# A three-stage transformer and Mamba kernel: norm weights folded into the MLP, W2 as three float32r products, the attention's last stores and two of its products moved

## The chip, the cores and the metric

The kernel runs on one core of one Trainium2 chip. The metric is the device time in microseconds. The core has TensorE (matmul), VectorE, ScalarE, GpSimd and SyncE (which here only issues DMA), each with its own queue of instructions; they wait for one another through semaphores. In the profile they are PE, DVE, ACT, POOL and SP; PEld is TensorE's load of a stationary operand, and a q behind a name is the engine's sequencer, where it issues a DMA.

## The reference

x has the shape (2, 64, 64, 256). Layer 0 is an attention over triples with an MLP, layer 1 a set of Mamba scans in both directions along rows and columns. The change touches layer 0 alone:

```python
out = jnp.einsum('biljh,bilhd,bljhd->bijhd', att, v1, v2)
attn_out = out.reshape(B, N, N, E) @ Wo
h = x_in + attn_out
h = _layer_norm(h, ln_agg_g, ln_agg_b)
mlp = jax.nn.relu(h @ W1 + b1) @ W2 + b2
h = mlp + h
return _layer_norm(h, ln_out_g, ln_out_b)
```

Here B = 2, N = 64, E = 256, 8 heads of d_k = 32, and W1 is 256 x 512. All is float32; the weights and biases of the norms are general, not ones and zeros.

## The kernel before

There are three blocks, one after the other, each ended by a barrier: `block_attention`, `block_mlp`, `block_mamba`.

**Attention.** The heads are taken in four pairs and the batch in two, so eight blocks c of 32 steps each; a step t makes the output rows of two i. In a step VectorE multiplies the attention weights by v2 for the first 22 of the 32 d (`DD = 22`, v2 in PSUM), GpSimd for the other ten (v2 in SBUF), both into `av[t % 2]` (line 338, `product`). TensorE multiplies that with block matrices of v1 (line 521, `rows`), in four strips of 8 d, into one of three PSUM banks. ScalarE evicts the bank into `ev` (line 699, `evict`) and, every four steps, builds the next matrices `w` (line 692). Four steps fill one half of `ev`; then SyncE stores it in 16 DMAs (`store`, line 279), one for each of 8 values d8 and 2 rows r. The very last group is stored in two parts: SyncE stores its first two steps in 16 DMAs and half of the d8 of the other two in 8; ScalarE issues the other 8 (`store_last`, line 753) after its last eviction. SyncE's queue is in order, so a group's stores start when those of the group before have been issued. Before this in ScalarE's queue, 13 loads for the MLP (`load_head`) are issued during the seventh block (c = 6).

**MLP.** The 8192 tokens are taken in 16 chunks c of 512. For a chunk TensorE multiplies by Wo (line 988), and VectorE adds x (line 1205), takes the moments and normalises (lines 1182, 1186, 1190, 1192), multiplies by the gain and adds the bias of the first norm (lines 1195, 1196), giving h. TensorE transposes h (line 999); ScalarE copies it as the high float32r part of hT (line 1098), VectorE subtracts that for the low part (line 1215). W1 is taken as three float32r products (line 1041: high by high, low by high, high by low), its own two parts made once by GpSimd (lines 951, 954). ScalarE applies b1 and the relu (line 1130), giving `hid`. W2 is one float32 product, which the profile shows as two records for each matmul (line 1053). VectorE adds b2 to h (line 1220), the product to that (line 1225), and does the second norm with gain and bias.

The order on the engines is written out by hand. VectorE: `front(c + 1)` (add x to first norm), then `back(c)` (b2, first half of the product, low part of hT for c + 1, second half, second norm). TensorE: Wo of c + 1, transposes of x1 for c - 2, W1 of c, the tiles t = 0, 1, 2 of W2 of c, the transposes of h for c + 1, the tile t = 3. ScalarE: copies of x1 for c - 2, the relus of c, with the square root for `front(c + 1)` behind the second, the copies of hT of c + 1, the square root for `back(c)`. SyncE loads and stores the chunks and, after chunks 2, 5 and 7, loads the input weights of the Mamba layers (`win`, which GpSimd splits) and the weights to be folded (`out_w`, `fcw`).

## Time and profile before

| | us |
|---|---|
| three runs, median | 2342.24 (2337.80 to 2343.77) |
| profiled execution | 2340.56 |
| its span | 2338.8 |
| PE, DVE busy | 1994.4 (85%), 1990.9 (85%) |
| ACT, POOL busy | 1264.6 (54%), 1336.7 (57%) |
| first row of the MLP block | 1084.56 |
| first row of the Mamba block | 1432.51 |

The profile is one execution. Busy shares are means over three stages with different limits, and a row of TensorE has a modelled end, so that pipelined rows overlap; the distance between starts tells the pace. The mean granted clock of TensorE is 0.978 of full speed (1.00 is 2.4 GHz, 0.50 is 1.2 GHz).

### The profile page before, as it was taken

What the parts mean: (1) busy time and instruction counts of PE and PEld (TensorE: products, weight loads), DVE (VectorE), ACT (ScalarE), POOL (GpSimd) and SP (SyncE); (2) the same over time, 40 slices, a digit from 0 to 9 for tenths busy, and PEclk for the clock granted to TensorE, in tenths of its full rate; (3) what the DMA queues carried; (4) which work ended last, traced back from release to release, by engine and by line L of the source; (5) the groups of instructions that cost most, each with busy time, mean ns of one, the idle gap of its engine ahead of it and who ended that gap; (6) DMA issues with size and microseconds to landing.
All of it is one profiled execution on the core that took longest, in us unless ns stands there. A gap on an engine that the chain in (4) does not pass through costs nothing. (4 is left out here: it accounts for less than half of the span.)

```text
span 2338.8 us, 43716 instructions
## 1 busy us (share of the span) xinstructions
PE 1994.4 (85%) x17008; PEld 1414.4 (60%) x17008; DVE 1990.9 (85%) x2292; ACT 1264.6 (54%) x3096; POOL 1336.7 (57%) x710
## 2 busy tenths in 40 slices
PE   8989976786687676664999997999999999999997
PEld 7868522242232221112787875888888888888886
DVE  4426799999999999994888884899899999999997
ACT  3337568858866882321232334656665655555652
POOL 1102699999989999992011001455655555666553
PEclk9999999999999999997999998999999999999997
DMA  7768512223231212300234222432223333433432
GB/s 234 249 207 243 151 34 57 48 50 59 62 56 21 38 29 58 71 11 24 64 105 142 71 64 62 73 83 75 73 73 85 84 82 99 102 91 95 104 93 64
DMA packets 300958, 204.00 MB, mean 87 GB/s; under 512 B 202192, under 2 KB 278992, under 8 KB 296656
## 3 DMA queue, kind: packets, MB, share of 16 engines
q1 hardware_dynamic: 282400, 146.51, 26.1%
q0 software_dynamic: 8704, 33.56, 3.9%
q10 hardware_dynamic: 9648, 21.14, 3.2%
q8 instruction: 135, 2.21, 0.4%
q14 instruction: 71, 0.58, 0.1%
HBM read 133.24 MB, written 67.90 MB: 86 GB/s over the span
## 5 line engine op out<-in xcount | busy, mean ns | idle before, releaser
L338 POOL TENSOR_TENSOR att_av<-att_att,att_v2sb 128x1280 f32<-128x1280 f32 (+1 forms) x256 | 764.6, 3003 | 43.2 <-PE att_bank L521 36.2
L338 DVE TENSOR_TENSOR att_av<-att_att,att_v2ps 128x2816 f32<-128x2816 f32 (+3 forms) x288 | 765.8, 2721 | 16.8 <-PE att_bank L521 13.6
L521 PE MATMUL att_bank<-att_av,att_w 128*32 128x512 f32 x4096 | 503.8, 601 | 224.0 <-DVE att_av L338 218.2
L521 PEld LDWEIGHTS att_bank<-att_av,att_w 128*32 128x32 f32 x4096 | 144.2, 109 | 522.5 <-issue 295.9
L1913 DVE SCALAR_TENSOR_TENSOR mb_cv<-mb_bank,mb_cw,mb_cv 128x504 f32<-128x504 f32 (+2 forms) x480 | 351.4, 732 | 60.3 <-ACT mb_cv L1707 48.8
L699 ACT ACTIVATE att_ev<-att_bank 128x512 f32<-128x512 f32 x256 | 151.8, 593 | 274.3 <-PE att_bank L521 263.5
L1512 POOL TENSOR_TENSOR mb_y_lo<-mb_y,mb_y_hi 128x1024 fp32r<-128x1024 f32 x60 | 142.6, 2398 | 258.7 <-DVE mb_S L1922 258.7
L1583 PE MATMUL mb_bank<-dt_xT_hi,dt_win_hi 128*128 128x512 f32 x576 | 233.8, 406 | 26.9 <-DVE mb_cv L1913 23.8
L1583 PE MATMUL mb_bank<-dt_xT_hi,dt_win_lo 128*128 128x512 f32 x576 | 226.3, 393 | 0.0
L1583 PE MATMUL mb_bank<-dt_xT_lo,dt_win_hi 128*128 128x512 f32 x576 | 226.2, 393 | 0.0
L1707 ACT ACTIVATE mb_cv<-mb_bank,mb_cw 128x512 f32<-128x512 f32 x160 | 110.2, 690 | 194.5 <-PE mb_bank L1583 193.0
L1518 POOL TENSOR_TENSOR mb_S<-mb_S,mb_dskip 128x512 f32<-128x512 f32 x124 | 158.1, 1294 | 9.7 <-DVE mb_S L1929 9.7
L1922 DVE TENSOR_TENSOR_SCAN mb_S<-mb_dAb,mb_inj 128x512 f32<-128x512 f32 x128 | 149.5, 1209 | 3.2 <-DMA mb_dAb<-dA_rows 3.2
L1583 PEld LDWEIGHTS mb_bank<-dt_xT_hi,dt_win_hi 128*128 128x128 f32 x576 | 109.4, 190 | 61.5 <-DVE mb_cv L1913 37.5
L1495 POOL TENSOR_TENSOR mb_inj<-mb_diag,dt_dt 128x512 f32<-128x512 f32 x128 | 129.6, 1045 | 13.1 <-DVE mb_S L1922 13.0
L1725 ACT ACTIVATE mb_xc<-mb_cv,mb_cb 128x512 f32<-128x512 f32 x128 | 91.5, 715 | 69.7 <-DVE mb_cv L1913 69.7
L1643 PE MATMUL mb_bank<-dt_wf_hi,mb_y_hi 128*128 128x256 f32 x512 | 128.7, 291 | 0.0
L642 ACT ACTIVATE att_raw<-att_raw,att_least 128x64 f32<-128x64 f32 x384 | 128.1, 336 | 0.4
L1643 PE MATMUL mb_bank<-dt_wf_lo,mb_y_hi 128*128 128x256 f32 x512 | 125.9, 285 | 0.0
L1583 PEld LDWEIGHTS mb_bank<-dt_xT_hi,dt_win_lo 128*128 128x128 f32 x576 | 109.0, 189 | 24.4
L1583 PEld LDWEIGHTS mb_bank<-dt_xT_lo,dt_win_hi 128*128 128x128 f32 x576 | 109.3, 190 | 19.7
L1053 PE MATMUL mlp_bank<-mlp_w,mlp_hid 128*128 128x256 f32 x512 | 118.4, 382 | 2.9 <-ACT mlp_hid L1130 2.9
(200 smaller groups left out, 3941.8 us busy)
## 6 DMA issues: line engine op xcount, KB each, us to landing
att_xin<-in_x SPq DMA_DIRECT2D x32, 512.0 KB, 4.5
qk_t<-att_qk POOLq DMA_DIRECT2D x16, 1024.0 KB, 5.1
v<-att_vs POOLq DMA_DIRECT2D x16, 1024.0 KB, 5.9
mb_dAb<-dA_rows SPq DMA_DIRECT2D x32, 512.0 KB, 6.3
mb_dAb<-dA_cols SPq DMA_DIRECT2D x32, 512.0 KB, 5.7
mixed_t<-att_ev SPq DMA_DIRECT2D x1008, 8.0 KB
att_q<-qk_t ACTq DMA_DIRECT2D x32, 256.0 KB, 4.4
att_kb<-qk_t ACTq DMA_DIRECT2D x64, 128.0 KB, 3.0
```

What stands on the lines that cost most here:

```text
L338: return eng.tensor_tensor(av[t % 2][:, :, d0:d1, :], a.unsqueeze(2).broadcast_to((P, 2, d1 - d0, N)), v2.unsqueeze(1).broadcast_to((P, 2, ...
L521: mm = pe.matmul(bank[t % NB][s * M:(s + 1) * M, :], w[k % 2][:, i0 // 2, r, s, :], av[t % 2][:, r, s * STRIP_D:(s + 1) * STRIP_D, :], sta ...
L642: ins = act.activation(a, a, ACT.Exp, scale=-1.0, bias=least[:, j, h:h + 1], accum_out=rsum[:, j, h:h + 1])
L699: act.activation(ev[e % 2][:, step % EB, :], bank[t % NB][:, :], ACT.Copy).then_inc(o_copied, 1)
L1053: mm = pe.matmul(OUT_[t // 2][:, (t % 2) * E:(t % 2 + 1) * E], hid[:, k, t * P:(t + 1) * P], w2[:, k, :], start=(i == 0), stop=(i == FT - 1))
L1495: pool.tensor_tensor(inj[:, p], diag[:, :].unsqueeze(1).broadcast_to((P, NH, L)), dtt[way(c)][:, c % NCHUNK * PAIR + p, :].unsqueeze(2).br ...
L1512: pool.tensor_tensor(y_["lo"][:, s, :], y[:, s, :], y_["hi"][:, s, :], ALU.subtract).then_inc(y_lo_ready, 1)
L1518: pool.tensor_tensor(S[:, p, :], S[:, p, :], dskip[way(c)][:, :, :].rearrange("p h t -> p (h t)"), ALU.add)\
L1583: mm = pe.matmul(PR_[b][:, :], win_[w][:, k, col:col + P], xT_[x][:, k, :], start=(n == 0), stop=(n == 3 * KT - 1))
L1643: pe.matmul(O_[t][:, 0:E], y_["hi"][:, m, t * P:(t + 1) * P], wf[way(c)][wn][:, m, :], start=(m == 0 and wn == "hi"), stop=False)
L1913: dve.scalar_tensor_tensor(out=dst, in0=src, scalar=cw[way(c)][:, m, TAPS - 1 - back:TAPS - back], in1=dst, op0=ALU.mult, op1=ALU.add)\
L1922: dve.tensor_tensor_scan(S[:, p, :], dAb[:, p, :], inj[:, p].rearrange("p h t -> p (h t)"), 0.0, ALU.mult, ALU.add).then_inc(scanned, 1)
```

## The change

In the attention's last block (c = 7), ScalarE makes the products of the last two d (`NA = 2`), during the steps from 6 on of the block before, into the memory of q and kb, which is free by then; GpSimd leaves these two out, and VectorE takes 21 d rather than 22 at every odd step but the first and last. TensorE then multiplies strip 3 in a part of six d and two of one. The last stores are shared differently: the second to last group is split by r between SyncE and ScalarE (8 DMAs each), and each of the last four steps is stored by itself, four DMAs from SyncE and four from ScalarE, which it issues between its evictions.

In the MLP, the gain g1 and bias be1 of the first norm are folded: W1 is scaled by g1 along its rows, be1 times W1 is added to b1 (by TensorE, once), and the residual is h * g1 + (b2 + be1), h now being without them. W2 is split into two float32r parts and hid too: ScalarE applies the relu twice (high part, float32), and VectorE subtracts. Some tiles share memory (`w1g` lies in `win`, the fold weights in w1, w2 and `win`), with waits for it on SyncE.

```diff
+            if t // (N // 2) == NC - 1 and 0 < t % (N // 2) < N // 2 - 1:
+                return DD - 1 - t % 2
             return DD
         def d_of_pool(t):
-            return DK
+            return DK - (NA if t // (N // 2) == NC - 1 else 0)
...
+                    n_av = STRIP_D - (NA if s == STRIPS - 1 and c == NC - 1 else 0)
                     for r in (0, 1):
-                        mm = pe.matmul(bank[t % NB][s * M:(s + 1) * M, :],
+                        mm = pe.matmul(bank[t % NB][s * M:(s + 1) * M, 0:n_av * N],
                                        w[k % 2][:, i0 // 2, r, s, :],
-                                       av[t % 2][:, r, s * STRIP_D:(s + 1) * STRIP_D, :], start=(r == 0), stop=(r == 1))
+                                       av[t % 2][:, r, s * STRIP_D:s * STRIP_D + n_av, :], start=(r == 0), stop=(r == 1))
+                    for a in range(STRIP_D - n_av):
+                        if step == 0 and a == 0:
+                            pe.wait_ge(av_by_act, NA)
+                        for r in (0, 1):
+                            mm = pe.matmul(bank[t % NB][s * M:(s + 1) * M, (n_av + a) * N:(n_av + a + 1) * N],
+                                           w[k % 2][:, i0 // 2, r, s, :],
+                                           by_act[a][:, 2 * step + r, :], start=(r == 0), stop=(r == 1))
...
             def store(c, e):
+                if c * NE + e == NC * NE - 1:
+                    for step in range(N // 2 - EB, N // 2):
+                        sp.wait_ge(o_copied, c * (N // 2) + step + 1)
+                        for d8 in range(STRIP_D // 2):
+                            store_step(sp, step, d8)
+                    return
+                sp.wait_ge(o_copied, c * (N // 2) + (e + 1) * EB)
+                for d8 in range(STRIP_D):
+                    for r in range(1 if c * NE + e == NC * NE - 2 else 2):
+                        store_rows(sp, c, e, d8, r)
...
+            def products(step):          # ScalarE, behind evict, block NC - 2
+                lo = 3 * (step - FIRST)
+                if step == FIRST:
+                    act.wait_ge(scored, PAIRS * NG)
+                    act.wait_ge(v2_loaded, NC * 32)
+                for j in range(max(0, lo), min(lo + 3, N)):
+                    for a in range(NA):
+                        ins = act.activation(by_act[a][:, :, j], att[(PAIRS - 1) % 2][:, (B - 1) * N:B * N, j], ACT.Copy,
+                                             scale=v2in[:, j, DK - NA + a:DK - NA + a + 1])
+            def store_last(step):        # ScalarE, behind evict, block NC - 1
+                if step == N // 2 - EB - 1:
+                    act.wait_ge(o_copied, NC * (N // 2) - EB)
+                    for d8 in range(STRIP_D):
+                        store_rows(act, NC - 1, NE - 2, d8, 1)
+                if step >= N // 2 - EB:
+                    act.wait_ge(o_copied, (NC - 1) * (N // 2) + step + 1)
+                    for d8 in range(STRIP_D // 2, STRIP_D):
+                        store_step(act, step, d8)
...
+            pool.wait_ge(cols_loaded, 32)
             for k in range(KT):
-                pool.tensor_copy(w1_["hi"][:, k], w1[:, k]).then_inc(w1_split, 1)
+                pool.tensor_tensor(w1g[:, k], w1[:, k], g1c[:, k:k + 1].broadcast_to((P, F)), ALU.mult).then_inc(w1_scaled, 1)
+            for k in range(KT):
+                pool.wait_ge(w1_scaled, k + 1)
+                pool.tensor_copy(w1_["hi"][:, k], w1g[:, k]).then_inc(w1_split, 1)
...
+            pool.tensor_copy(w2_["hi"][:, :, :], w2[:, :, :]).then_inc(w2_split, 1)
+            pool.wait_ge(w2_split, 1)
+            pool.tensor_tensor(w2_["lo"][:, :, :], w2[:, :, :], w2_["hi"][:, :, :], ALU.subtract).then_inc(w2_split, 1)
...
                 for t in range(TT):
-                    for i, k in enumerate(ORDER):
-                        if t == 0:
+                    for n, (hn, wn, i, k) in enumerate([(hn, wn, i, k) for hn, wn in (("hi", "hi"), ("hi", "lo"), ("lo", "hi"))
+                                                        for i, k in enumerate(ORDER)]):
+                        if t == 0 and n < FT:
                             pe.wait_ge(hid_ready, FT * c + i + 1)
-                        mm = pe.matmul(OUT_[t // 2][:, (t % 2) * E:(t % 2 + 1) * E], hid[:, k, t * P:(t + 1) * P],
-                                       w2[:, k, :], start=(i == 0), stop=(i == FT - 1))
+                        if t == 0 and hn == "lo":
+                            pe.wait_ge(hid_lo_ready, FT * c + i + 1)
+                        mm = pe.matmul(OUT_[t // 2][:, (t % 2) * E:(t % 2 + 1) * E], hid_[hn][:, k, t * P:(t + 1) * P],
+                                       w2_[wn][:, k, :], start=(n == 0), stop=(n == 3 * FT - 1))
...
             times_wo(0, 0)
+            pe.wait_ge(cols_loaded, 32)
+            for m in range(FT):
+                for k in range(KT):
+                    mm = pe.matmul(OUT_[0][:, m:m + 1], w1[:, k, m * P:(m + 1) * P], be1c[:, k:k + 1],
+                                   start=(k == 0), stop=(k == KT - 1))
+            mm.then_inc(b1_done, 1)
...
-                    act.activation(hid[:, m, :], HID_[m][:, :], ACT.Relu, bias=b1[:, m:m + 1]).then_inc(hid_ready, 1)
+                    act.activation(hid_["hi"][:, m, :], HID_[m][:, :], ACT.Relu, bias=b1f[:, m:m + 1])
+                    act.activation(hid[:, m, :], HID_[m][:, :], ACT.Relu, bias=b1f[:, m:m + 1]).then_inc(hid_ready, 1)
...
+            def low_of_hid(c):
+                for i, m in enumerate(ORDER):
+                    dve.wait_ge(hid_ready, FT * c + i + 1)
+                    dve.tensor_tensor(hid_["lo"][:, m, :], hid[:, m, :], hid_["hi"][:, m, :], ALU.subtract)\
+                        .then_inc(hid_lo_ready, 1)
...
             def front(c, u):
-                layer_norm(0, c, chain, h[u], h[u], row["g1"], row["be1"], h_ready)
+                normed_rows(0, c, chain, h[u], h[u]).then_inc(h_ready, 1)
...
             def back(c, u):
-                dve.tensor_tensor(hb[u][:, :, :], h[u][:, :, :], wide(row["b2"]), ALU.add).then_inc(b2_added, 1)
+                dve.tensor_tensor(hb[u][:, :, :], h[u][:, :, :], wide(row["g1"]), ALU.mult).then_inc(h_scaled, 1)
+                dve.wait_ge(h_scaled, c + 1)
+                dve.tensor_tensor(hb[u][:, :, :], hb[u][:, :, :], wide(row["b2"]), ALU.add).then_inc(b2_added, 1)
...
             for c in range(NCHUNK):
                 if c + 1 < NCHUNK:
                     front(c + 1, 1 - c % 2)
+                low_of_hid(c)
                 back(c, c % 2)
```

## Rows read from the trace of the kernel before

**Rows 1.** Busy us by window: PE, PEld, DVE, ACT, POOL, clock, DMA; MLP
```profile
1200.00:1450.00 250.00, 232.38 (x1270) 189.62 (x1268) 197.91 (x434) 88.85 (x187) 18.95 (x18) 0.97 0.28 87
```

**Rows 2.** Timeline of TensorE, two chunks: start, length, operation, idle before
```profile
1248.20 4.73 PE L1053 MATMUL mlp_bank<-mlp_w,mlp_hid 128*128 128x256 f32 x20 [0.28 <-ACT mlp_hid L1130]
1252.77 1.04 PE L999 MATMUL mlp_bank<-mlp_ident,mlp_h 128*128 128x128 f32 x8
...
1276.70 5.27 PE L988 MATMUL mlp_bank<-mlp_wo,mlp_att 128*128 128x256 f32 x16 [2.46 <-DMA mlp_xin<-in_x]
```

**Rows 3.** Timeline of VectorE, one chunk
```profile
1243.99 1.28 DVE L1205 TENSOR_TENSOR mlp_h<-mlp_bank,mlp_xin 128x512 f32<-128x512 f32 x2
...
1249.31 1.22 DVE L1195 TENSOR_TENSOR mlp_h<-mlp_h,mlp_g 128x1024 f32<-128x1024 f32 x1
1250.56 1.22 DVE L1196 TENSOR_TENSOR mlp_h<-mlp_h,mlp_be 128x1024 f32<-128x1024 f32 x1
1251.82 1.22 DVE L1220 TENSOR_TENSOR mlp_hb<-mlp_h,mlp_b 128x1024 f32<-128x1024 f32 x1
1253.08 0.69 DVE L1225 TENSOR_TENSOR mlp_hb<-mlp_bank,mlp_hb 128x512 f32<-128x512 f32 x1
1254.03 1.29 DVE L1215 TENSOR_TENSOR mlp_hT_lo<-mlp_bank,mlp_hT_hi 128x512 fp32r<-128x512 f32 x2 [0.26 <-ACT mlp_hT_hi L1098]
1255.57 0.69 DVE L1225 TENSOR_TENSOR mlp_hb<-mlp_bank,mlp_hb 128x512 f32<-128x512 f32 x1 [0.25 <-PE mlp_bank L1053]
...
1262.69 1.28 DVE L1205 TENSOR_TENSOR mlp_h<-mlp_bank,mlp_xin 128x512 f32<-128x512 f32 x2
```

**Rows 4.** Timeline of ScalarE, same chunk
```profile
1247.48 1.25 ACT L1130 ACTIVATE mlp_hid<-mlp_bank,mlp_b 128x512 f32<-128x512 f32 x2
```

**Rows 5.** Timeline of TensorE in the Mamba block, a float32r product of 256 columns
```profile
1605.35 2.08 PE L1650 MATMUL mb_bank<-dt_wf_hi,mb_y_lo 128*128 128x256 f32 x16
```

**Rows 6.** Groups on VectorE: count, busy us, mean ns, idle before
```profile
L1952 DVE TENSOR_TENSOR mb_sq<-mb_sq 128x512 f32<-128x512 f32 x32 | 22.2, 692 | 1.1
```

**Rows 7.** Timelines of VectorE, SyncE and ScalarE at the attention's end
```profile
1047.87 18.20 DVE L338 TENSOR_TENSOR att_av<-att_att,att_v2ps 128x2816 f32<-128x2816 f32 x8
...
1056.75 25.51 SPq L279 DMA_DIRECT2D mixed_t<-att_ev  x40
...
1068.25 0.60 ACT L699 ACTIVATE att_ev<-att_bank 128x512 f32<-128x512 f32 x1 [2.53 <-PE att_bank L521]
1068.87 1.20 ACTq L753 DMA_DIRECT2D mixed_t<-att_ev  x1
1068.87 6.18 ACTq L753 DMA_DIRECT2D mixed_t<-att_ev  x8
1084.56 0.10 POOL L947 MEMSET mlp_eps<- 128x1 f32 x1 [19.46 <-POOLq L2072]
```

**Rows 8.** Timeline of ScalarE in the attention, scaled copies of 64 elements
```profile
859.90 2.01 ACT L654 ACTIVATE att_raw<-att_raw,att_rsum 128x64 f32<-128x64 f32 x8
```

**Rows 9.** Timeline of the MLP's first chunk
```profile
1086.52 2.49 POOL L954 TENSOR_TENSOR mlp_w_lo<-mlp_w,mlp_w_hi 128x512 fp32r<-128x512 f32 x2
...
1098.07 1.23 DVE L1196 TENSOR_TENSOR mlp_h<-mlp_h,mlp_be 128x1024 f32<-128x1024 f32 x1
1099.35 1.97 PE L999 MATMUL mlp_bank<-mlp_ident,mlp_h 128*128 128x128 f32 x8 [8.65 <-DVE mlp_h L1196]
```

**Rows 10.** Timelines of VectorE and GpSimd while GpSimd splits the input weights
```profile
1231.33 3.67 POOL L965 CAST dt_win_hi<-mlp_win 128x1152 fp32r<-128x1152 f32 x2 [48.34 <-DMA mlp_win<-in_mv_in_wT]
1231.95 2.05 DVE L1220 TENSOR_TENSOR mlp_hb<-mlp_h,mlp_b 128x1024 f32<-128x1024 f32 x1
```

**Rows 11.** Busy us by window, with the granted clock ahead of the DMA share
```profile
1058.00:1064.00 6.00, 3.90 (x38) 1.14 (x34) 6.00 (x4) 1.19 (x2) 5.87 (x3) 1.00 0.06 13
1277.00:1279.00 2.00, 2.00 (x6) 1.55 (x6) 1.56 (x5) 0.27 (x1) 0.00 (x0) 0.50 0.01 4
```

**Rows 12.** Timeline of TensorE, W2 of the last chunk
```profile
1404.55 7.07 PE L1053 MATMUL mlp_bank<-mlp_w,mlp_hid 128*128 128x256 f32 x32
```

88 lines of the change are left out of this document (57 added, 31 removed).

## The prediction

> **What bounds the kernel now.** I read the busy table by stage first, then the timelines of single chunks on each engine, then the queues. The page gives TensorE 85% and VectorE 85% of the span, which says nothing of a stage; the windows over the MLP do: of 250 us, TensorE is busy 232 and VectorE 198 [rows 1]. So TensorE looks like the bound, and the timeline of one chunk is needed. VectorE's loop runs from one add of Wo's product to the next, 1243.99 to 1262.69, 18.70 us, with its instructions back to back but for short waits, among them 0.26 before the low part of hT and 0.25 before the second half of W2's product [rows 3]. TensorE's work comes to nearly the same and has 0.28 us of idle time [rows 2]; its busy share is also made of modelled matmul ends. The reader should see here two engines of equal length where the order on VectorE closes the loop. An instruction added to VectorE lengthens a chunk; time taken from TensorE alone doesn't shorten it.
>
> At the end of the attention it is another resource. VectorE's product for two i takes 3.0 us a step when a few are followed (18.20 us over the last, merged), and the last eviction starts at 1068.25, but SyncE issues 40 stores in 25.51 us from 1056.75 to 1082.26, 0.64 us each, and the MLP's first row is at 1084.56 [rows 7]. Its queue, not the arithmetic, ends that stage.
>
> **The change, part by part.** Sums are against the profiled execution, 2340.56 us (span 2338.8 and 1.76 around it); the median of the three runs is 2342.24, 1.68 above it.
>
> *Attention, last block of 32 steps.* ScalarE makes the products of two of the 32 d, GpSimd two fewer, VectorE one fewer (21 for 22) at the 15 odd steps between first and last. One d of 22 is 1/22 of 3.0 us = 0.136; 15 x 0.136 = -2.0 us. GpSimd's share falls from 10 d to 8 or 9, so it stays below VectorE. ScalarE's 128 activations of 64 elements lie in the block before, six a step; eight comparable ones take 2.01 us [rows 8], so 1.5 us a step beside an eviction of 0.60 and now and then a build, in 3 us: hidden, at most a step late now and then, with three PSUM banks as cover (0 to +1 us). TensorE adds eight short records a step to a step with 1 us of slack: 0.
>
> *The tail's stores.* Count from the end of the eviction of step 27, when the second to last group of stores starts (1056.75). Before, SyncE has 16 + 16 + 8 issues: 25.5 us. After, it has 8, then 4 behind each of the steps 28 to 31; ScalarE has 8, then 4 behind each of its evictions, and its next eviction stands behind those issues in order. ScalarE's eight issues took 6.18 us with SyncE's beside them, the first 1.2 [rows 7], so one costs 0.7 and the first of a group 0.5 more. ScalarE: 8 issues 1.2 + 7 x 0.67 = 5.9 us, then four times (eviction 0.62 + issues 1.2 + 3 x 0.66) = 3.8 us, end at 21.1. SyncE's last four wait for the eviction of step 31 at 18 and end at 20.5. The gain is 25.5 - 21.1 = 4.4 us. Bounds: if evictions came on time (12.1 us after step 27), SyncE would end at about 14.7, a gain of 10.8; if ScalarE's issues all cost 0.75, it is 3. I take -4.3, since the queue order is certain.
>
> *MLP, start.* The first norm's gain and bias are gone: 2.5 us of the way to the first transposes, which begin at 1099.35, behind the bias at 1098.07 [rows 9]. Ahead of it GpSimd now waits for two small loads, scales W1 (two of its 512-wide operations, 2.49 us [rows 9]), splits it, and splits W2 (twice the width): from the loads' landing some 11 us, before either is wanted, since the transposes and a product with Wo stand ahead. TensorE's 16 records for b1 fall in its idle time before 1099.35. But GpSimd now works beside the first norm, and VectorE's operation on two SBUF tensors rose to 2.05 us from 1.22 when GpSimd ran [rows 10, 3]. I add 1.0 (0 to 2.5): -1.5 in all.
> The Trainium skill, "GPSIMD Engine Reference", Specifications, says the same of the pair: it shares its SBUF interfaces with VectorE, and they contend when VectorE has two SBUF inputs. By it the new subtraction, SBUF alone, is exposed too, where the loads of W_in are split; the trace bears it out for the same kind of operation, and it would add under 1 us there.
>
> *MLP, each chunk on TensorE.* W2 was 32 records of 256 columns a chunk, 7.07 us [rows 12], 0.217 each. It becomes 48 float32r records. The same form (stationary 128x128, 256 columns, float32r) runs 16 in 2.08 us, 0.12 each [rows 5]: 48 x 0.12 = 5.8. TensorE gains 1.2 us a chunk. Were the weight load, whose record lasts 0.19, to set the pace, it would lose 2.2.
>
> *MLP, each chunk on VectorE.* Removed: gain and bias of the first norm, 1249.31 to 1251.82, 2.51 us. Added: h times g1, 1.26, and four subtractions of 512. The nearest row is a 512-wide operation from SBUF, 692 ns alone [rows 6]; back to back two of that size take 1.28 to 1.30 [rows 3], so 0.60 each, 2.45 with the last's end. Net +1.2.
>
> *The order.* The subtractions stand between front(c+1) and back(c), and TensorE can't pass its first tile of W2 before the last of them; h of chunk c+1 is transposed two tiles later. Call T the end of the last subtraction. TensorE: 0.15, then 12 + 12 records at 0.12, so the transposes start at T + 3.05; from the start of the transposes to the low part of hT is 1.26 (1252.77 to 1254.03 [rows 2, 3]): T + 4.3. VectorE has 1.26 + 1.26 + 0.69 = 3.2 us of work until then, and waits 1.1 us where it waited 0.26. The loop, from the add of Wo's product: front without gain and bias 7.83 - 2.51 = 5.32; subtractions 2.45; to the low part of hT 4.3; from there to the next add 1262.69 - 1254.03 = 8.66, less the wait of 0.25 that may fall away, 8.5. Sum 20.6 us against 18.70: +1.9. ScalarE's four extra relus, 0.56 each [rows 4], fit: the square root of the next norm stands between them, at about T - 4.3, and after it come four passes of 0.56, so the last hid is ready near T - 2, before VectorE asks for it. If that were late by one pass it would cost 0.5.
> From the second add to the last there are 13 such periods, and one of start-up that TensorE sets (+0.7): 13 x 1.9 + 0.7 = +25.4.
>
> *What stalls the loop now and won't then.* At 1276.70 TensorE waited 2.46 us for a load of x beside the fold weights, and its next 16 records took 5.27 us where 16 x 0.22 = 3.5 are due [rows 2]; 4.2 us in all. With 1.9 us more in a chunk the load is nearly in time: -3.5 (0 to -4).
>
> *End.* After the last front the chain is subtractions of chunk 14, W1, one pass of relu more, and three tiles of W2 at 1.44 each instead of the whole at 0.217: +1.5.
>
> *TensorE's clock.* After the wait of 2.46 us it was granted 0.50, its lower level of 1.2 GHz; in the attention, busy 3.90 of 6 us, it kept 1.00 [rows 11, 2]. The new loop leaves TensorE 3 us of idle time a chunk, in pieces of 1.0, 1.0, 0.3 and 0.5 us with single records between, all in the 4 us ahead of T. That stands between the two rows. A fall costs about 1.4 us of the loop, since it hits the way from T to the transposes. I count one or two chunks: +2.
>
> Sum: -2.0 - 4.3 - 1.5 + 25.4 - 3.5 + 1.5 + 2.0 = +17.6; 2340.56 + 17.6 = 2358.2 profiled, and 2342.24 + 17.6 = 2359.8 as a median. I say 2360.
>
> **Rivals.**
> 1. *The clock falls in most chunks.* The low part's late arrival makes TensorE run single records with gaps for 4 us, every chunk at the same place. 13 to 14 chunks x 1.4 = 19, less the 2 counted: 2377. For it: the half clock behind one gap of 2.46 us. Against: the attention's regular gaps. 0.13.
> The Trainium skill, "TensorE: Matmul & The Clock Gate", section "A second HAM failure mode: psum-queue depth-cycling", describes it: frequent short idles between groups of matmuls make the clock switch to and fro. By that rule this rival holds; the attention's rows don't bear it out.
> 2. *The other side: the stores pay for the loop.* If ScalarE's issues return at once, so that its evictions aren't held, the tail gives 10.8 rather than 4.3; and if TensorE's first tile overtakes so that VectorE has no stall at the low part of hT, the loop grows by the net work of 1.2 alone. The place that decides is the queue of ScalarE behind step 27: the kernel isn't slower from the point where the tail gives 10 us and a chunk costs no more than 1.2. Then -2.0 - 10.8 - 2.5 + 13 x 1.2 + 0.7 - 3.5 + 1.5 = -1.0: 2341. For it: both queues idle otherwise. Against: issue durations are on ScalarE's row. 0.15.
> 3. *TensorE is the bound after all.* Then a chunk shrinks by 1.2: 15 x -1.2 = -18, with -2.0 - 4.3 - 1.5: 2316. For it: 232 of 250 us busy. Against: VectorE's loop has no room for 1.2 more. 0.05.
> 4. *The weight load paces the three products.* 48 x 0.19 = 9.1 a chunk; three tiles at 2.3 before and behind the transposes put 1.7 us more ahead of the low part and as much behind: 15 x 2.5 = 37 more, 2397. Against: the row at 0.12. 0.03.
> 5. *The change doesn't do what it says*, a part of its tail or its products on ScalarE falling on the path (c = 6 evictions late by a step each time): +5 to +10, 2367. 0.06, inside the range.
>
> **How the numbers follow.** Forecast 0.58, rivals 0.13, 0.15, 0.05, 0.03, 0.06. A change under 0.3% (7 us) can't be told from none: 2335.2 to 2349.3. Faster: rival 3 and a part of 2, 0.08. Same: the rest of 2 and the lower edge of the forecast, 0.14. Slower: 0.78. The forecast's own range is 2350 to 2369 (tail 3 to 10.8, stall 0.8 to 1.4 a chunk, start 0 to 2.5). The range that holds 8 in 10 reaches to the edge of rival 2 and to rival 1: 2343 to 2379.
>
> **What would show it.** Right: the add of Wo's product every 20.4 to 20.8 us; W2's records 0.12 apart; VectorE idle 1.1 us ahead of the low part of hT on ScalarE's copy; subtractions 0.6 apart; the MLP's first row 6 us earlier, at 1078; ScalarE's evictions of steps 28 to 31 each 3.8 us apart. Wrong: a pitch of 18.7 or less (TensorE was the bound), of 22 with half clock ahead of the transposes (rival 1), or a first row of the MLP before 1073 (rival 2).

## The result and the profile after

The changed kernel takes 2358.56 us as a median of four runs (2357.69 to 2362.40), the kernel before 2340.99 in runs beside it (2337.80 to 2343.77): ratio 1.0079, 95% interval 1.0064 to 1.0094, so 18.5 us slower. The forecast was 2360. Two executions used below stood far outside the others, one of kernel 3 (3271 us at a mean granted clock of 0.55) and one of the kernel before beside kernels 9 to 12 (3406 us at 0.64); the ratios leave them out, the printed median of 3 counts its own. The profiled execution took 2357.77 us with a span of 2356.0, which is 17.2 us above the profiled one of before; the ledger below is made between those two.

| stretch (profiled executions) | before | after | measured | forecast |
|---|---|---|---|---|
| attention to the eviction of step 27 | 1056.12 | 1050.30 | -5.8 | -2.0 |
| from there to the MLP's first row | 28.4 | 24.1 | -4.3 | -4.3 |
| MLP's first row to the second add of Wo's product | 21.73 | 20.38 | -1.35 | -1.5 |
| second to last such add, 14 chunks | 274.45 | 301.09 | +26.6 | +25.4 - 3.5 + 2.0 = +23.9 |
| last add to Mamba's first row | 51.77 | 55.75 | +4.0 | +1.5 |
| Mamba | 906.3 | 904.3 | -1.9 | 0 |

A chunk of the MLP on VectorE, timeline of the kernel after (start, length, group, idle time ahead and who ended it), which answers to [rows 3]:

```profile
1289.34 1.28 DVE L1295 TENSOR_TENSOR mlp_h<-mlp_bank,mlp_xin 128x512 f32<-128x512 f32 x2
...
1293.23 1.38 DVE L1278 TENSOR_SCALAR mlp_h<-mlp_h,mlp_mv,mlp_rstd 128x256 f32<-128x256 f32 x4
1294.64 2.50 DVE L1285 TENSOR_TENSOR mlp_hid_lo<-mlp_hid,mlp_hid_hi 128x512 fp32r<-128x512 f32 x4
1297.06 1.22 DVE L1311 TENSOR_TENSOR mlp_hb<-mlp_h,mlp_g 128x1024 f32<-128x1024 f32 x1
1298.31 1.23 DVE L1313 TENSOR_TENSOR mlp_hb<-mlp_hb,mlp_b 128x1024 f32<-128x1024 f32 x1
1299.57 0.69 DVE L1318 TENSOR_TENSOR mlp_hb<-mlp_bank,mlp_hb 128x512 f32<-128x512 f32 x1
1301.55 1.29 DVE L1306 TENSOR_TENSOR mlp_hT_lo<-mlp_bank,mlp_hT_hi 128x512 fp32r<-128x512 f32 x2 [1.29 <-ACT mlp_hT_hi L1181]
...
1309.91 1.28 DVE L1295 TENSOR_TENSOR mlp_h<-mlp_bank,mlp_xin 128x512 f32<-128x512 f32 x2
```

The reader should see the forecast's path in it: 20.57 us from add to add (20.6 forecast, 18.70 before), the subtractions in 2.50, and a wait of 1.29 us (1.1 forecast, 0.26 before) for the high part of hT. The same chunk on TensorE, which answers to [rows 2]:

```profile
1295.27 0.39 PE L1129 MATMUL mlp_bank<-mlp_w_hi,mlp_hid_hi 128*128 128x256 f32 x1 [0.77 <-ACT mlp_hid L1216]
1295.50 0.64 PE L1129 MATMUL mlp_bank<-mlp_w_lo,mlp_hid_hi 128*128 128x256 f32 x4
...
1297.20 0.38 PE L1129 MATMUL mlp_bank<-mlp_w_hi,mlp_hid_lo 128*128 128x256 f32 x1 [0.22 <-DVE mlp_hid_lo L1285]
1297.42 0.63 PE L1129 MATMUL mlp_bank<-mlp_w_hi,mlp_hid_hi 128*128 128x256 f32 x4
1297.89 0.64 PE L1129 MATMUL mlp_bank<-mlp_w_lo,mlp_hid_hi 128*128 128x256 f32 x4
...
1300.29 1.03 PE L1070 MATMUL mlp_bank<-mlp_ident,mlp_h 128*128 128x128 f32 x8
```

Four records every 0.47 to 0.48 us, 0.12 each as forecast, and the transposes 3.15 us behind the end of the last subtraction at 1297.14 (3.05 forecast). That pace holds at full clock. In four chunks it is 0.85 us for four records over a stretch; windows of the kernel after at such a place, over the loop, and over the loop of the kernel with fillers described below (columns as in [rows 1], the granted clock behind POOL):

```profile
1254.90:1258.10 3.20, 3.20 (x17) 3.20 (x16) 2.27 (x3) 0.00 (x0) 0.00 (x0) 0.50 0.00 0
1096.00:1395.00 299.00, 268.72 (x1661) 223.75 (x1659) 253.28 (x567) 117.23 (x239) 26.29 (x12) 0.98 0.27 84
```
```profile
1094.00:1390.00 296.00, 286.37 (x1927) 248.17 (x1925) 255.13 (x568) 118.24 (x241) 26.67 (x12) 1.00 0.27 85
```

The granted clock falls to 0.50 (1.2 GHz) four times in the loop of 14 chunks, at 1125.1, 1189.9, 1254.8 and 1360.6; before, once, at 1276.5. VectorE in the chunk of the third fall:

```profile
1251.62 2.50 DVE L1285 TENSOR_TENSOR mlp_hid_lo<-mlp_hid,mlp_hid_hi 128x512 fp32r<-128x512 f32 x4
...
1260.03 1.29 DVE L1306 TENSOR_TENSOR mlp_hT_lo<-mlp_bank,mlp_hT_hi 128x512 fp32r<-128x512 f32 x2 [2.37 <-ACT mlp_hT_hi L1181]
```

From the end of the last subtraction to the low part of hT it is 5.91 us, against 4.41 in the chunk at 1289.34 (4.3 forecast). So it is in all four: 5.70, 5.91, 5.91 and 5.91, while nine of the other ten chunks have 4.41 or 4.42 and one 4.81. A fall in the loop lengthens this one path, by 1.3 to 1.5 us.

The attention's end on ScalarE and SyncE, and the MLP's first row, which answer to [rows 7]:

```profile
1050.30 0.60 ACT L729 ACTIVATE att_ev<-att_bank 128x512 f32<-128x512 f32 x1 [2.14 <-PE att_bank L551]
1050.92 6.56 ACTq L235 DMA_DIRECT2D mixed_t<-att_ev  x8
1057.59 0.60 ACT L729 ACTIVATE att_ev<-att_bank 128x512 f32<-128x512 f32 x1 [6.69 <-issue]
1058.21 2.92 ACTq L242 DMA_DIRECT2D mixed_t<-att_ev  x4
1061.18 0.60 ACT L729 ACTIVATE att_ev<-att_bank 128x512 f32<-128x512 f32 x1 [3.00 <-issue]
...
1069.00 2.91 ACTq L242 DMA_DIRECT2D mixed_t<-att_ev  x4
```
```profile
1050.92 5.38 SPq L235 DMA_DIRECT2D mixed_t<-att_ev  x8
1058.21 13.32 SPq L242 DMA_DIRECT2D mixed_t<-att_ev  x16
```
```profile
1074.43 0.10 POOL L1011 MEMSET mlp_eps<- 128x1 f32 x1 [16.12 <-POOLq L2172]
```

The evictions of steps 28 to 31 stand behind ScalarE's issues (the idle time ahead of them is "issue"), 3.59 us apart where 3.8 was forecast. SyncE's row of 16 is merged and holds three waits of about 1 us for the next eviction; its first four alone:

```profile
1058.21 2.55 SPq L242 DMA_DIRECT2D mixed_t<-att_ev  x4
```

VectorE's products in the last block, groups by form (count, busy us, mean ns):

```profile
L359 DVE TENSOR_TENSOR att_av<-att_att,att_v2ps 128x2688 f32<-128x2688 f32 x15 | 44.3, 2955 | 0.0
L359 DVE TENSOR_TENSOR att_av<-att_att,att_v2ps 128x2560 f32<-128x2560 f32 x15 | 42.3, 2822 | 0.0
...
L359 DVE TENSOR_TENSOR att_av<-att_att,att_v2ps 128x2816 f32<-128x2816 f32 x1 | 3.1, 3090 | 0.0
```

2816, 2688 and 2560 elements are 22, 21 and 20 d. This shows that my working, and the text ahead of it, misread one line: `DD - 1 - t % 2` gives VectorE 21 d at even steps and 20 at odd ones, not 22 and 21, so that GpSimd has 9 and 10 and not 8 and 9. Its ten d take 2.93 us (groups of 1280 elements), a little over VectorE's 2.82 for twenty.

### The profile page after: what moved, and what is told of

Read it like the earlier page. It is cut to its first block and busy times, and to the rows that moved or that the text cites. A ratio compares the mean times of both kernels' runs of the same rounds, so it can differ in the third digit from the quotient of the medians.

```text
span 2356.0 us, 45040 instructions
## 1 busy us (share of the span) xinstructions
PE 2000.0 (85%) x17536; PEld 1445.9 (61%) x17536; DVE 2003.7 (85%) x2342; ACT 1339.0 (57%) x3288; POOL 1337.4 (57%) x714
## 5 line engine op out<-in xcount | busy, mean ns | idle before, releaser
L359 POOL TENSOR_TENSOR att_av<-att_att,att_v2sb 128x1280 f32<-128x1280 f32 (+3 forms) x256 | 759.3, 2985 | 41.7 <-PE att_bank L544 34.7
L359 DVE TENSOR_TENSOR att_av<-att_att,att_v2ps 128x2816 f32<-128x2816 f32 (+4 forms) x288 | 759.9, 2702 | 15.8 <-PE att_bank L544 12.6
L544 PE MATMUL att_bank<-att_av,att_w 128*32 128x512 f32 (+1 forms) x4096 | 502.9, 598 | 216.7 <-DVE att_av L359 204.5
L1595 POOL TENSOR_TENSOR mb_inj<-mb_diag,dt_dt 128x512 f32<-128x512 f32 x128 | 129.8, 1048 | 13.0 <-DVE mb_S L2022 12.9
L1730 PEld LDWEIGHTS mb_bank<-mb_S,mb_xtok 64*64 64x64 f32 x4096 | 107.9, 137 | 13.4 <-issue 10.9
```

The lines of the kernel that those rows point to most:

```text
L359: return eng.tensor_tensor(av[t % 2][:, :, d0:d1, :], a.unsqueeze(2).broadcast_to((P, 2, d1 - d0, N)), v2.unsqueeze(1).broadcast_to((P, 2, ...
L544: mm = pe.matmul(bank[t % NB][s * M:(s + 1) * M, 0:n_av * N], w[k % 2][:, i0 // 2, r, s, :], av[t % 2][:, r, s * STRIP_D:s * STRIP_D + n_a ...
L1595: pool.tensor_tensor(inj[:, p], diag[:, :].unsqueeze(1).broadcast_to((P, NH, L)), dtt[way(c)][:, c % NCHUNK * PAIR + p, :].unsqueeze(2).br ...
```

## The experiments

Each kernel is the one before or the changed one with the edit given. Each ratio is taken to runs of the kernel before beside that kernel (medians 2339.34 for 1 to 4, 2340.99 for 5 to 8, 2340.94 for 9 to 12); time to the kernel before is the ratio less 1, times 2341. A pitch is the time from the first add of Wo's product of one chunk to that of the next, and the usual pitch is what most undisturbed chunks have. "Loop" is from the second to the last add of Wo's product, 14 chunks, in the profiled execution; "falls" is how often the granted clock went to 0.50 within it. In the expectations, theory A is the account that I held before the run.

| kernel | median us | ratio (95%) | to before | loop | usual pitch | falls |
|---|---|---|---|---|---|---|
| before | 2340.99 | 1 | | 274.5 | 18.70 | 1 |
| changed | 2358.56 | 1.0079 (1.0064 to 1.0094) | +18.5 | 301.1 | 20.59 | 4 |
| 1 attention alone | 2329.93 | 0.9957 (0.9943 to 0.9971) | -10.1 | 275.0 | 18.70 | 1 |
| 2 stores alone | 2335.41 | 0.9982 (0.9972 to 0.9991) | -4.2 | 274.4 | 18.70 | 1 |
| 3 MLP alone | 2374.62 | 1.0137 (1.0117 to 1.0158) | +32.1 | 308.3 | 20.57 or 22.07 | 8 |
| 4 fold alone | 2333.41 | 0.9975 (0.9965 to 0.9984) | -5.9 | 270.7 | 18.70 | 0 |
| 5 split of W2 alone | 2441.30 | 1.0430 (1.0415 to 1.0444) | +100.7 | 370.6 | 24.4 to 26.1 | 14 |
| 6 transposes early | 2345.39 | 1.0024 (1.0014 to 1.0033) | +5.6 | 290.5 | 19.72 | 3 |
| 7 fillers | 2355.32 | 1.0055 (1.0042 to 1.0068) | +12.9 | 296.0 | 20.58 | 0 |
| 8 low part on GpSimd | 2355.13 | 1.0060 (1.0048 to 1.0073) | +14.0 | 300.5 | 19.6 to 22.7 | 7 |
| 9 MLP alone, fillers | 2362.00 | 1.0084 (1.0070 to 1.0098) | +19.7 | 297.5 | 20.59 | 1 |
| 10 no subtractions | 2341.47 | 1.0001 (0.9992 to 1.0010) | +0.2 | 286.8 | 19.63 | 2 |
| 11 attention and fold | 2324.37 | 0.9926 (0.9913 to 0.9939) | -17.3 | 270.6 | 18.70 | 0 |
| 12 as 11, loads spread | 2322.00 | 0.9914 (0.9900 to 0.9928) | -20.1 | 269.3 | 18.70 | 0 |

**1 and 2: the attention's parts.** 1 has the changed `block_attention`, the whole of that part of the diff, and everything else as before. 2 takes this back of it, so that only the stores are changed:

```diff
-            if t // (N // 2) == NC - 1 and 0 < t % (N // 2) < N // 2 - 1:
-                return DD - 1 - t % 2
-            return DK - (NA if t // (N // 2) == NC - 1 else 0)
+            return DK
-                if c == NC - 2:
-                    products(step)
```

> Only the attention's edits (ScalarE's products of two d, one d fewer for VectorE and two for GpSimd, the last stores on two queues); the MLP as before. Theory A, from the profile of the changed kernel (VectorE's steps in the last block 2.80 us for 3.00, so -5.8; 23.5 us from the eviction of step 27 to the MLP for 27.8, so -4.3): -10, 2331. Rival, the terms as predicted (-2.0 and -4.3): -6.3, 2335. Rival, the attention's gain comes back as waits in the MLP: no change.

> Only the stores of the attention's end are shared between SyncE and ScalarE; nobody multiplies other d than before. Theory A: -4.3 us, with ScalarE's evictions of steps 28 to 31 some 3.6 us apart and 23.5 us from the eviction of step 27 to the MLP's first row. Rival: with steps of 3.0 us the evictions come later anyway, and the gain is 5 or more; or, if the two queues slow each other's issues, under 2.

Both came out as theory A has it, 2 by its trace above all (24.0 us from the eviction of step 27 to the MLP's first row, for 28.4 before), since its interval reaches from -6.6 to -2.1. The MLP's first row is at 1074.74 in 1, at 1080.70 in 2 and at 1084.56 before: 3.9 us for the stores and 6.0 for the steps. In 2 the evictions behind ScalarE's issues are 3.5 to 3.7 us apart, as in the changed kernel; by then the shorter steps don't matter.

**3 and 9: the MLP alone, and with fillers.** 3 is the changed kernel with the attention of before. 9 adds the fillers of 7:

```diff
+                        if t == 0 and c > 0 and n in FILL:      # {2: 7, 3: 7, 9: 2, 10: 2, 11: 2}
+                            for _ in range(FILL[n]):
+                                pe.matmul(OUT_[1][:, E:2 * E], hid_["hi"][:, ORDER[0], 0:P], w2_["hi"][:, 0, :],
+                                          start=True, stop=True)
                         if t == 0 and n < FT:
                             pe.wait_ge(hid_ready, FT * c + i + 1)
```

> Only the MLP's edits (norm folded, W2 as three float32r products); the attention as before. Theory A: loop +26.6, end +4.0, start -1.4, so +27 to +29: 2369. If the two parts add up, this one and the attention's alone make +17.6. Rival: the falls of TensorE's clock depend on when the MLP starts, and without them it is +20.

> The kernel with only the MLP's edits (before's attention), with the same fillers in TensorE's idle time. It had 9 falls of the clock in the loop and 308.3 us from the second add of Wo's product to the last, where the changed kernel with the same MLP had 4 and 301.1. Theory A (the falls are all that differs between those two loops): no falls, loop 296 as in the changed kernel with fillers, -12 us to 2374.6, 2362. Rival (something else of the attention's end is carried into the loop): loop 300 or more, 2367 to 2370.

3 was slower than expected by its middle value, 32.1 us over before; its interval, +27.4 to +37.0, still touches the expected +27 to +29. With the attention's -10.1 it makes +22.0 where both together have +18.5. Its MLP instructions are those of the changed kernel, yet its loop is 7.2 us longer. Eight stretches at half clock stand in it rather than four (the nine of the expectation above count one behind the last add), and undisturbed chunks with one take 22.07 instead of 20.57. The mean granted clock is 0.973 in each of the four executions behind its ratio, and 0.975 to 0.977 in the changed kernel's four, so this is not one odd profile. Windows over the loops of 3 and of 9:

```profile
1104.00:1410.00 306.00, 274.38 (x1662) 229.54 (x1661) 255.03 (x567) 116.16 (x238) 26.35 (x12) 0.95 0.27 82
```
```profile
1104.00:1401.00 297.00, 287.84 (x1924) 249.38 (x1923) 254.38 (x568) 118.76 (x242) 26.44 (x12) 0.99 0.27 85
```

With fillers one fall is left, in the first of the 14 chunks, and the loop takes 297.5: 10.8 us less for seven falls, and a median of 2362.0 where 2362 was expected. In chunks 3, 8, 12 and 14 of the loop a fall costs 1.48 to 1.50. Not all of the 10.8 is the clock: in chunk 4 of kernel 3, 23.54 us for 21.08 in 9, GpSimd splits `win` while VectorE subtracts, and the four subtractions take 3.45 us for 2.50. So the two loops of one MLP differed mostly by the clock, and by 1 to 2 us through this, chunk 5 being late too. Why the clock fell in other chunks when the MLP began 9.5 us later isn't settled.

**4: the fold alone.** The changed MLP with W2 and hid as they were, and the attention of before:

```diff
-                    act.activation(hid_["hi"][:, m, :], HID_[m][:, :], ACT.Relu, bias=b1f[:, m:m + 1])
-                low_of_hid(c)
...
-                        mm = pe.matmul(OUT_[t // 2][...], hid_[hn][:, k, t * P:(t + 1) * P], w2_[wn][:, k, :], ...)
+                        mm = pe.matmul(OUT_[t // 2][...], hid[:, k, t * P:(t + 1) * P], w2[:, k, :], ...)
```

> Only the first norm's gain and bias are folded into W1 and b1; W2 stays one float32 product, and there is no low part of hid; the attention as before. VectorE's chunk loses 2.51 us and gains 1.26 (h times g1): 18.70 - 1.25 = 17.45 us; TensorE's work of 18.4 us a chunk would bind then. Theory A: pitch 18.4 to 18.5, -3 us over the loop, -1.4 at the start, and the stall at the fold weights' load stays: -4 to -6, 2336. Rival (VectorE's loop alone set the pace): -1.25 x 14 - 1.4 = -19, 2323. Rival: no change, since gaps move elsewhere.

Theory A holds as far as the sum goes; its pitch was to fall to 18.4 or 18.5 and stayed at 18.70. That the loop is 3.7 us shorter all the same comes from chunks that stood out before (22.81 to 21.07 us at the late load of x, 20.19 to 19.15, 19.88 to 19.25), so the sum was met in part by luck. TensorE's waits over 14 chunks, of this kernel and of the one before (total, times, longest), and one chunk's rows on VectorE here:

```profile
PE mlp_bank L1069 <- ACT mlp_hid L1155: 2.3, 4, 1.4
PE mlp_bank L1004 <- DMA mlp_xin<-in_x: 2.3, 1, 2.3
```
```profile
PE mlp_bank L1053 <- ACT mlp_hid L1130: 2.9, 6, 1.4
PE mlp_bank L988 <- DMA mlp_xin<-in_x: 2.5, 1, 2.5
```
```profile
1250.53 1.29 DVE L1245 TENSOR_TENSOR mlp_hT_lo<-mlp_bank,mlp_hT_hi 128x512 fp32r<-128x512 f32 x2 [1.52 <-ACT mlp_hT_hi L1121]
```

With 1.25 us of VectorE's work gone, VectorE waits 1.52 us where it waited 0.26, and the chunk is as long as before. VectorE's work didn't set the pitch, then. TensorE waited 6.2 us in the 14 chunks before and 4.6 here, next to nothing: it was the bound of the loop before, with VectorE, which waited 0.26 and 0.25 us in a chunk [rows 3], close behind. No run shortened TensorE's work alone, so TensorE's part rests on these waits.

**5: the split alone.** The changed MLP with W1 and b1 unscaled and the attention of before, and

```diff
-                normed_rows(0, c, chain, h[u], h[u]).then_inc(h_ready, 1)
+                chain.link(normed_rows(0, c, chain, h[u], h[u]))
+                chain.link(dve.tensor_tensor(h[u][:, :, :], h[u][:, :, :], wide(row["g1"]), ALU.mult))
+                dve.tensor_tensor(h[u][:, :, :], h[u][:, :, :], wide(row["be1"]), ALU.add).then_inc(h_ready, 1)
...
-                dve.tensor_tensor(hb[u][:, :, :], h[u][:, :, :], wide(row["g1"]), ALU.mult).then_inc(h_scaled, 1)
```

> Only W2 as three float32r products with the subtractions on VectorE; the first norm keeps gain and bias, the attention is as before. Theory A (the path from the last subtraction over three tiles of W2 and the transposes to the low part of hT sets the chunk): 7.83 to the end of the norm, 2.45 of subtractions, 4.3 to the low part of hT, 8.5 to the next add, 23.1 us, with 2.4 us of waiting ahead of the low part: +4.4 x 14 = +62 and what falls of TensorE's clock add, 2405. Rival (VectorE's work alone counts, its waits being slack): 18.7 + 2.45 - 0.26 = 20.9 us, +31, 2370.

Slower than both. The clock fell in all 14 chunks, and for longer. The window over the loop, then two rows that stand side by side in the fourth chunk:

```profile
1106.00:1470.00 364.00, 301.17 (x1641) 248.36 (x1640) 277.29 (x570) 113.88 (x234) 26.18 (x12) 0.86 0.22 69
```
```profile
1198.76 3.10 DVE L1223 TENSOR_TENSOR mlp_hid_lo<-mlp_hid,mlp_hid_hi 128x512 fp32r<-128x512 f32 x1
1198.26 3.06 POOL L985 TENSOR_TENSOR dt_win_lo<-mlp_win,dt_win_hi 128x1152 fp32r<-128x1152 f32 x1
```

Theory A's path is there piece by piece: 7.83 to the subtractions in ten of the 14 chunks, 2.50 for them in twelve, 8.36 from the low part of hT to the next add in eight and at most 9.15 in the others. With 4.42 from the last subtraction to the low part of hT that makes 23.1, and 14 x 23.1 = 323 of the 370.6 us. The other 47 us are in three places. From the last subtraction to the low part of hT it is 5.7 to 7.2 us in every chunk, partly at half clock, 28 us in all over 14 x 4.42. In chunks 4 and 7 GpSimd splits `win` beside the subtractions, which take 9.10 and 6.80 us for 2.50, 11 us more in all. The last 8 us are elsewhere, 3.6 of them in the first chunk. That the 28 us are the clock's rests on the length of the same path at full clock in the changed kernel, 4.41; no run took the falls away here.

**6: transposes early.** The changed kernel with

```diff
-                    if t == 2:
-                        turn_h(c + 1, 1 - u)
+                        if t == 0 and n == 2 * FT:
+                            turn_h(c + 1, 1 - u)
                         if t == 0 and hn == "lo":
```

> The changed kernel, but h of the next chunk is transposed in the first tile of W2, ahead of its four products with the low part of hid, not behind the third tile. Theory A: VectorE's wait of 1.29 us ahead of the low part of hT goes, its own work of 19.3 us a chunk is what is left: pitch 19.3 to 19.5 for 20.59, 14 x 1.2 = -17 to the changed kernel, 2342. Rival (TensorE's queue sets the pace): the transposes delay the first tile by as much as they bring, pitch 20.2 or more, 2353 to 2359.

Pitch 19.72, a little over theory A's, and 13 us faster than the changed kernel (5.6 over before for 18.5), where theory A had 17. Rows of a chunk:

```profile
1252.20 1.28 DVE L1306 TENSOR_TENSOR mlp_hT_lo<-mlp_bank,mlp_hT_hi 128x512 fp32r<-128x512 f32 x2
1253.96 0.69 DVE L1318 TENSOR_TENSOR mlp_hb<-mlp_bank,mlp_hb 128x512 f32<-128x512 f32 x1 [0.48 <-PE mlp_bank L1131]
```

The wait of 1.29 is gone and one of 0.48 for the second half of W2's product has come: 1.29 - 0.48 = 0.8, near the 0.87 that the pitch fell by.

**7: fillers.** The changed kernel with the edit of 9.

> The changed kernel with idle TensorE time ahead of the subtractions' end filled: 7, 7, 2, 2 and 2 products of 256 columns a chunk whose result is overwritten, put before the waits. Theory A (the falls of the clock to 0.50 in the loop cost 1.5 us each and come from that idle time): no falls in the loop, -6 us to the changed kernel, 2353. Rival: the falls stay and the fillers in front of a product cost up to 0.1 us a chunk, 2359 to 2361.

No falls, and the loop 5.1 us shorter, 1.3 for each of the four falls. The median is 3.2 us lower, the ratio 5.6, and the intervals of the ratios overlap; that TensorE's idle time caused the falls rests on the granted clock and on 9, where the difference is four times as large.

**8: the low part on GpSimd.** The changed kernel; the subtractions moved to GpSimd, and (the edits on GpSimd, SyncE and in VectorE's `low_of_hid` are left out here)

```diff
+                products(0, 0, 2 * FT)                  # tile, from product, to product
+                products(2, 0, 2 * FT)
+                turn_h(c + 1, 1 - u)
+                products(0, 2 * FT, 3 * FT)
+                products(1, 0, 3 * FT)
+                products(2, 2 * FT, 3 * FT)
+                products(3, 0, 3 * FT)
...
+                low_of_hT(c + 1, 1 - u)                 # VectorE, ahead of both adds
                 for half in range(2):
                     dve.wait_ge(w2_done, 2 * c + half + 1)
```

> The changed kernel with the subtractions for hid's low part on GpSimd, the products with the high part of hid of tiles 0 and 2 ahead of the transposes of h, and these ahead of all products with the low part; the low part of hT comes ahead of both adds of W2's product; GpSimd's split of W_in is spread over chunks 4 to 12 and its loads moved behind it (W_in's second at chunk 7, the fold weights at 12). Theory A: VectorE loses 2.45 us a chunk, and the chain norm, relus, GpSimd's last subtraction, products, add, norm makes 18.0 us: -2.6 x 14 = -36 to the changed kernel, 2322. Rival (VectorE's operations on two SBUF tensors slow down beside GpSimd, 2.05 us for 1.22, for two or three a chunk): pitch 19.5 to 20.5, 2343 to 2357.

The rival by the time, though the pitch is 19.6 to 22.7 for its 19.5 to 20.5, with seven falls of the clock among them. VectorE and GpSimd side by side, first in a chunk where GpSimd also casts a part of `win`, then in one where it only subtracts:

```profile
1207.52 2.33 DVE L1296 TENSOR_SCALAR mlp_h<-mlp_h,mlp_mv,mlp_rstd 128x256 f32<-128x256 f32 x4
1209.89 2.19 DVE L1323 TENSOR_TENSOR mlp_hb<-mlp_h,mlp_g 128x1024 f32<-128x1024 f32 x1
1212.12 2.05 DVE L1325 TENSOR_TENSOR mlp_hb<-mlp_hb,mlp_b 128x1024 f32<-128x1024 f32 x1
```
```profile
1208.43 2.57 POOL L1048 TENSOR_TENSOR mlp_hid_lo<-mlp_hid,mlp_hid_hi 128x512 fp32r<-128x512 f32 x2 [1.64 <-ACT mlp_hid L1234]
1210.95 2.14 POOL L1038 CAST dt_win_hi<-mlp_win 128x1152 fp32r<-128x1152 f32 x1
```
```profile
1120.56 2.34 DVE L1296 TENSOR_SCALAR mlp_h<-mlp_h,mlp_mv,mlp_rstd 128x256 f32<-128x256 f32 x4
1122.93 2.19 DVE L1323 TENSOR_TENSOR mlp_hb<-mlp_h,mlp_g 128x1024 f32<-128x1024 f32 x1
1125.15 1.23 DVE L1325 TENSOR_TENSOR mlp_hb<-mlp_hb,mlp_b 128x1024 f32<-128x1024 f32 x1
```

In the first, VectorE's three operations take 6.57 us for 3.84 alone (1.38 + 1.23 + 1.23), 2.7 more: it gives back the 2.50 us that moved. In the second it is 1.9 more, from the subtractions alone. Eight of the chunks have a part of `win` beside them. The run changed the order on TensorE and the loads of `win` too, so how its time divides between this and the seven falls isn't shown.

**10: no subtractions.** The changed kernel with

```diff
-                low_of_hid(c)
...
-                        mm = pe.matmul(OUT_[t // 2][...], hid_[hn][:, k, t * P:(t + 1) * P], w2_[wn][:, k, :], ...)
+                        mm = pe.matmul(OUT_[t // 2][...], hid_["hi"][:, k, t * P:(t + 1) * P], w2_[wn][:, k, :], ...)
```

> The changed kernel without the four subtractions a chunk: the third product of W2 reads the high part of hid again, so its result isn't the reference's; TensorE and ScalarE do the same work. Theory A (a path through VectorE's norm, ScalarE's relus, three tiles of W2 and the transposes): the transposes start 1.2 to 1.5 us earlier in a chunk and not 2.45, pitch 19.0 to 19.5, -16 to -20 us to the changed kernel, 2340. Rival (only VectorE's work counts): pitch 18.1, -35, 2324. Rival (TensorE's work binds): 17.5 to 17.7, 2317.

Pitch 19.63, just above theory A's range, and neither rival's. A chunk on VectorE:

```profile
1308.39 0.69 DVE L1316 TENSOR_TENSOR mlp_hb<-mlp_bank,mlp_hb 128x512 f32<-128x512 f32 x1 [1.02 <-PE mlp_bank L1127]
1310.83 1.29 DVE L1304 TENSOR_TENSOR mlp_hT_lo<-mlp_bank,mlp_hT_hi 128x512 fp32r<-128x512 f32 x2 [1.75 <-ACT mlp_hT_hi L1179]
```

Taking away 2.50 us of VectorE's work brings 0.96 of pitch; VectorE waits 2.77 us for the path through ScalarE and TensorE. So even free subtractions leave the loop 0.93 us a chunk slower than before, though W2's products are cheaper on TensorE. What is left in that path is ScalarE; its queue in the chunk above:

```profile
1302.86 0.30 ACT L1174 ACTIVATE mlp_std<-mlp_mv,mlp_eps 128x4 f32<-128x4 f32 x1 [0.61 <-DVE mlp_mv L1270]
...
1304.77 0.70 ACT L1214 ACTIVATE mlp_hid<-mlp_bank,mlp_b1f 128x512 f32<-128x512 f32 x1
```

The square root waits for VectorE's moments, and four passes of relu stand behind it in the queue; TensorE's last wait of the chunk ends with the fourth, at 1305.5, and three tiles of W2 come ahead of the transposes. Before, it was two passes. TensorE waited 18.8 us in the loop for hid, 24 times, against 2.9 before; the sum is the same in the changed kernel, so it shows ScalarE late in both but not by itself what sets the pitch. Neither a single relu pass nor another place of the square root was tried.

**11 and 12: what remains worth doing.** 11 has the attention's edits and the fold of 4. 12 also spreads the fold weights' loads:

```diff
-                if c == 7:
-                    for d in range(2):
-                        for dst, src in (...):
-                            sp.dma_start(dst, src).then_inc(fold_w_loaded, 16)
+                if 7 <= c <= 12:
+                    dst, src = [...][c - 7]
+                    sp.dma_start(dst, src).then_inc(fold_w_loaded, 16)
```

> The attention's edits and the norm's fold, W2 left one float32 product. If the parts add up: -10.3 (attention alone) and -5.9 (fold alone) to before: 2324. Rival (the clock or the load of x at the fold weights is hit otherwise by the earlier start): 2327 to 2330.

> As the attention's edits with the fold and float32 W2, and the six loads of fold weights go one behind each of the stores of chunks 7 to 12 instead of all behind chunk 7. Theory A: the late load of x (2.3 to 2.5 us of waiting on TensorE, 2.4 us of one chunk with the norm folded) goes: -2.4, 2321. Rival: the loads collide later, or the wait was hidden: no change, 2324.

The parts add: -10.1 and -5.9 alone, -17.3 together (-20.4 to -14.3). In 11 TensorE still waits for x, in 12 that line is gone from its waits:

```profile
PE mlp_bank L1053 <- DMA mlp_xin<-in_x: 2.2, 1, 2.2
```

The chunk with the late load took 20.95 us in 11 and 18.70 in 12, while the loop is 1.3 us shorter, since its first chunk is 0.9 longer. The medians differ by 2.4 as theory A has it, but their intervals overlap, so only the trace shows it. 12 has the lowest median of this study, 20 us under the kernel before. 11 differs from the changed kernel by the split of W2 alone: 18.5 + 17.3 = 36 us is what the split costs there. Without the attention's edits it is 32.1 + 5.9 = 38 us on top of the fold, but 101 us without the fold (5): with gain and bias of the first norm still in front of the subtractions, the path is 2.5 us longer in a chunk, the clock falls in every one, and the subtractions meet GpSimd's split of `win`.

## Why the prediction was right, point by point

The time was right, and so were the path that sets the loop and most of the terms. That the profiled sum came within 0.4 us (17.2 for 17.6) is luck: the steps (-3.8) and Mamba (-1.9) came out below their terms, the loop (+2.7) and the end (+2.5) above.

- *VectorE's loop, 20.6 us for 18.70.* Right, by 20.57 and by its inner marks. Without falls of the clock the loop of 7 is 296.0 - 274.45 = 21.5 us longer; the forecast without its term for the clock was 25.4 - 3.5 = 21.9. The path from the last subtraction over three tiles and the transposes (4.41 us for 4.3) is confirmed by 6, which shortened it, and by the chunks with a fall, which are longer on this path and by as much.
- *W2's records at 0.12.* Right; rival 4 is out. What the forecast said beside it, that the order on VectorE closes the loop of the kernel before, was wrong: 4 shows TensorE as its bound. The error did no harm since the new path is longer than either engine's work. Rival 3 read TensorE's busy share rightly and still failed, because the new path doesn't let TensorE profit.
- *ScalarE's extra relus cost nothing.* True only while VectorE's subtractions are later: in the chunk at 1289.34 the last relu ends 1.9 us before the last subtraction, 2 as forecast. 10 shows the next path, through hid's waits, 0.93 us above the old pitch.
- *The tail's stores, -4.3.* Right (-4.3 here, -4.2 alone in 2). The four evictions held behind ScalarE's issues are the row that rival 2 needed to be otherwise.
- *The last block's steps, -2.0.* The step that failed: "VectorE one fewer (21 for 22) at the 15 odd steps". It is 21 or 20 at 30 steps, on average 1.5 d fewer; 30 x 1.5 x 0.136 = -6.1 by the same price, -5.8 measured. The MLP's first row, forecast at 1078, came at 1074.43 by this.
- *The MLP's start, -1.5.* Near, -1.35. The parts by themselves are further off and don't add up to it: -1.85 with the attention of before (3), +1.2 with only the attention changed (1), which the forecast didn't have. *The stall at the fold weights.* Gone as forecast: no wait for x is left in TensorE's list in the loop of the changed kernel. It was close: 6, whose chunks are 0.9 us shorter, has one of 1.3 us, 10 one of 1.5, and 7, with the same pitch and no falls of the clock, one of 0.8.
- *GpSimd beside the new subtraction, under 1 us.* Right by luck. In the changed kernel GpSimd's split of `win` fell beside other operations (2.05 to 2.17 us for 1.23); begun elsewhere, the subtractions met it and took 0.95 us more in 3 and 10.9 in 5. One row of before could have warned of `tensor_scalar`, too: 2.28 us at 1239.13 for 1.38, beside GpSimd.
- *The clock, +2.0.* The mechanism and the price of a fall were right (1.4; 1.3 and 1.5 in 7 and 9), the count was not: four falls, 5.1 us. Rival 1 had the chance 0.13, and it nearly came in 3, the same MLP begun later: 8 falls of 14 chunks. What I had held against it, that the attention keeps its clock with regular gaps [rows 11], did not carry over to gaps of about 0.8 us with single records between. TensorE's waits ahead of T were 1.7 us a chunk (24.5 in 14), not the 3 forecast.
The Trainium skill, "TensorE: Matmul & The Clock Gate", section "A second HAM failure mode: psum-queue depth-cycling", has short idles between groups of matmuls make the clock go to and fro. The rows of 3 and 5 agree with it (8 and 14 falls), and so does their near absence in 7 and 9 (0 and 1). But in the changed kernel TensorE's waits from the last hid on are the same in the chunk at 1289 and in the one before the fall at 1254.8 (0.77, then about 0.22 twice), and only the second has a fall, so the rule alone doesn't tell the count.
- *The end, +1.5.* Mis-sized, +4.0. From the last add of Wo's product to the last low part of hT it is 16.9 us for 11.7 before, of which about 2.2 is the longer path of that chunk (12.2 for 10.0 in an ordinary one), which my 13 periods didn't hold; the clock was at 0.50 from 1404.9 on, in the middle of it. Behind that the end is 1.2 us shorter. In 7 and 9, with the falls elsewhere, the end is 56.7 and 56.6, so how its 4.0 us divide stays open.
- *Mamba, 0.* Its time was 1.9 us shorter, with the same code. Over the 14 kernels profiled here it lies between 904.3 and 907.2 us, so this is spread.

## What to carry to other kernels

Before cheapening a product on the busiest engine, follow the path that its new inputs need through the other engines: here TensorE saved about 1.3 us a chunk, while the second relu and the subtraction stood between two engines in series, and the pitch rose by 1.9, half of it with the subtractions (10). Undo a change by halves before judging it: its attention part and the fold alone make the kernel 17 us faster, and W2's split takes all of that back and more. Where an engine ahead of the critical product runs in short bursts, count the falls of the granted clock in the profile, and expect their number to depend on when the stage starts.
